# Masked keys by GpSimd instead of DMA, five normalisations moved to GpSimd, and values formed by head parity, in a four-block transformer kernel

## The reference

```python
x = _L0_xcond_ref(x, cond, ctx, ...)    # norm, attention over ctx (1 head), router of 3 experts, gate
x = _L1_xcond_ref(x, cond, ctx, mask, ...)  # norm, self attention, norm, cross attention, norm, MLP
x = _L2_xcond_ref(x, cond, ctx, ...)    # the same with other details; ctx is normalised too
x = _L3_xcond_ref(x, cond, ctx, ...)    # the same with rotary queries and keys

# inside blocks 1 to 3, self attention (cross attention takes keys and values from ctx):
q, k, v = split(xn @ qkv_w + qkv_b)               # 16 heads of 8 features
w = softmax(einsum('bqhd,bkhd->bhqk', q, k) * scale)
out = einsum('bhqk,bkhd->bqhd', w, v) @ proj_w
x = x + gate * out
```

## Time and profile before

| | us |
|---|---|
| median of 3 runs | 2580.94 |
| lowest, highest | 2578.9, 2584.88 |
| the profiled execution | 2582.11 |
| its span, from first to last instruction | 2580.3 |

### The profile page before, as it was taken

The page is one execution under the profiler, slowest core; times in us unless marked ns, Lnnn a source line. Parts: engine busy times, 40 slices in busy tenths (PEclk is TensorE's granted clock), DMA queues, the critical chain, the costliest instruction groups (busy, mean ns, idle before and its releaser), DMA issues.

```text
span 2580.3 us, 79116 instructions
## 1 busy us (share of the span) xinstructions
PE 2315.9 (90%) x32156; PEld 1821.8 (71%) x32156; DVE 2078.1 (81%) x4845; ACT 1904.0 (74%) x4567; POOL 70.0 (3%) x100
## 2 busy tenths in 40 slices
PE   3989899999989999899999889998899999998897
PEld 3767677767776777767777667776677777776675
DVE  4697878878788887788877988878887888787885
ACT  2678767777777877678777777777786887776875
POOL 0000000000000000000000000000000000000000
PEclk9999999999999999999999999999999999999998
DMA  6100000000100000000000000010001000000000
GB/s 135 39 14 21 14 22 26 31 16 13 30 21 30 15 17 27 27 23 15 18 30 30 13 20 20 27 30 13 20 20 31 30 15 15 26 18 22 12 12 16
DMA packets 99458, 62.90 MB, mean 24 GB/s; under 512 B 32992, under 2 KB 94368, under 8 KB 99104
## 3 DMA queue, kind: packets, MB, share of 16 engines
q1 hardware_dynamic: 90592, 57.80, 7.6%
q10 hardware_dynamic: 8512, 0.03, 0.2%
HBM read 28.31 MB, written 4.29 MB: 13 GB/s over the span
## 4 chain that ended last, share of the span: by engine, by line
PE 45%; DVE 31%; ACT 11%; DMA 5%; issue 4%; SPq 2%; DVEq 0%; ACTq 0%
PE pair L806 9%; DVE mx L1020 8%; DVE wide L1022 7%; PE pair L843 7%; PE pair L783 6%; PE pair L828 5%; PE pair L859 4%; PE pair L864 4%; DVE wide L1016 3%; DVE stats L900 2%; DMA wide<-probs_by_expert 2%; ACT xn L936 2%; PE pair L878 2%; DVE wide L918 2%; DVE x L1050 2%
## 5 line engine op out<-in xcount | busy, mean ns | idle before, releaser
L966 ACT ACTIVATE wide<-pair 128x1024 f32<-128x1024 f32 x384 | 390.3, 1022 | 122.6 <-PE pair L843 119.5
L1020 DVE TENSOR_REDUCE mx<-pair 128x16 f32<-128x1024 f32 x320 | 389.5, 1217 | 82.2 <-PE pair L828 81.5
L843 PE MATMUL pair<-konst,wide 128*128 128x128 f32 x3072 | 405.7, 276 | 54.8 <-DVE wide L1022 42.0
L843 PEld LDWEIGHTS pair<-konst,wide 128*128 128x128 f32 x3072 | 342.5, 142 | 120.5 <-DVE wide L1022 78.4
L1022 DVE TENSOR_TENSOR wide<-pair,mx 128x1024 f32<-128x1024 f32 x320 | 391.9, 1225 | 10.9
L936 ACT ACTIVATE xn<-pair,table 128x64 f32<-128x64 f32 x896 | 287.7, 406 | 46.3 <-PE pair L927 44.9
L828 PE MATMUL pair<-km,qT 32*64 32x256 f32 x6144 | 221.5, 394 | 94.5 <-DMA km<-kT 24.8
L959 ACT ACTIVATE vb<-pair 64x128 f32<-64x128 f32 x768 | 207.2, 270 | 38.1 <-PE pair L813 23.2
L918 DVE TENSOR_SCALAR wide<-x,mv,rstd 128x128 f32<-128x128 f32 x640 | 191.3, 343 | 50.9 <-ACT rstd L911 47.3
L828 PEld LDWEIGHTS pair<-km,qT 32*64 32x64 f32 x6144 | 125.8, 133 | 149.6 <-issue 20.6
L859 PEld LDWEIGHTS pair<-wide,vb 128*32 128x32 f32 x12288 | 184.0, 110 | 53.9 <-issue 17.6
(11 more groups left out here) (219 smaller groups left out, 4315.0 us busy)
## 6 DMA issues: line engine op xcount, KB each, us to landing
km<-kT SPq DMA_DIRECT2D x768, 32.0 KB, 1.8
wide<-probs_by_expert SPq DMA_DIRECT2D x32, 256.0 KB, 2.9
x<-in_x_dram SPq DMA_DIRECT2D x32, 128.0 KB, 2.4
ctx<-in_ctx_dram SPq DMA_DIRECT2D x32, 128.0 KB, 2.3
wide<-probs_by_expert SPq DMA_DIRECT2D x32, 128.0 KB, 3.2
out_dram<-x SPq DMA_DIRECT2D x32, 128.0 KB, 1.9
w0e<-in_L_xcond_e_w_dram SPq DMA_DIRECT2D x4, 384.0 KB, 5.8
w1fc<-in_L_xcond_fc_w_dram SPq DMA_DIRECT2D x2, 256.0 KB, 4.9
```

What stands on the lines that cost most here:

```text
L843: ins = pe.transpose(b[:, t:t + 128], G.ss[:, 2 * c + rr, a:a + 128], ident)
L966: act.activation(G.pT[:, :, 4 * c:4 * c + 4, :].rearrange("k p h q -> k p (h q)"), two_banks(name)[:].rearrange("k (p n) -> k p n", p=2), ...
L1020: dve.tensor_reduce(top, heads(s), AX_X, ALU.max).then_inc(*tick("dve", ("max", G.n, tag, c)))
```

## The change

1. The masked keys are made by GpSimd: `pool_keys` (step `kp`) multiplies `kT` by a column of 0s and 1s (`K_OWN + j` in `konst`) into each of the four copies, in place of the four DMAs. `keys_in` is gone; `pe_scores` and `copied_before` wait for GpSimd's tick ("keys").
2. `pool_apply` does the two `tensor_scalar` of the normalisations 1b, 2b, 3b, 2c and 0 on GpSimd. The other six stay on VectorE.
3. `pe_values` forms values per sequence and head parity: eight products of 128 x 64 with 64 columns (a strided view of the weights), odd heads into partitions 64 to 127. `act_values` then needs two ScalarE instructions of 64 x 256.
4. The costs given to the steps, and `hop`, are other numbers, and all of `PLACES` is another order. Of its lines, those of the steps `km` or `kp` and `s` of tag 1s stand for the rest (one number a visit).

```diff
-PE_MM, PE_TURN, PE_SCORES, PE_MIX = 0.44, 0.12, 1.05, 1.95
+PE_MM, PE_TURN, PE_SCORES, PE_MIX = 0.45, 0.12, 1.07, 1.915
...
-    "km1s": "185 234 275 276 995 1105 1279 1395 1971 2089 2255 2369 2947 3067 3241 3353 3932 4049 4217 4329 4911 5020 5197 5317 5891 6005 6174 6290 6870 6982 7153 7266",
-    "s1s": "188 251 279 306 1002 1112 1284 1399 1981 2093 2264 2378 2965 3073 3242 3361 3946 4051 4227 4341 4926 5031 5204 5321 5904 6015 6185 6302 6885 6992 7157 7277",
...
+    "s1s": "158 247 290 317 1002 1224 1272 1328 1979 2202 2253 2310 2959 3182 3231 3289 3939 4164 4214 4271 4919 5141 5195 5252 5901 6122 6173 6232 6880 7098 7150 7207",
+    "kp1s": "155 232 268 280 991 1210 1240 1318 1971 2199 2222 2299 2949 3174 3208 3278 3929 4152 4187 4261 4911 5139 5165 5241 5889 6112 6131 6220 6870 7092 7125 7194",
...
-NK = K_ONE + 3 * PV
+K_OWN = K_ONE + 3 * PV
+NK = K_OWN + 4
...
+    k[p, K_OWN + p % JH] = 1
...
         def pe_values(pe, G, tag, src, w):
 
             b = claim(pe, (G.n, tag, "v"))
-            for p in range(TT):
-                ins = pe.matmul(b[:, p * D:(p + 1) * D], src[:, p * 128:(p + 1) * 128], w, start=True, stop=True)
+            parity = w.rearrange("f (g e d) -> f g e d", e=2, d=HD)
+            for b2 in range(2):
+                for p in range(TT):
+                    tok, a = (2 * p + b2) * S, (b2 * TT + p) * S
+                    for e in range(2):
+                        ins = pe.matmul(b[S * e:S * e + S, a:a + S].rearrange("k (g d) -> k g d", d=HD), src[:, tok:tok + S],
+                                        parity[:, :, e, :], start=True, stop=True)
             ins.then_inc(*tick("pe", ("mm", (G.n, tag, "v"))))
 
         def pe_scores(pe, G, tag):
 
             pe.wait_ge(*done("qT", G.n, tag))
-            pe.wait_ge(keys_in[G.stream], 16 * JH * copies(G, tag))
+            pe.wait_ge(*done("keys", G.n, tag))
...
+        on_pool = ("1b", "2b", "3b", "2c", "0")
...
+        def pool_apply(pool, G, tag):
+
+            x, _, mv, rstd, out = norm_of(G, tag)
+            pool.wait_ge(*done("rstd", G.n, tag))
+            for t in range(TT):
+                pool.tensor_scalar(out[:, t, :], x[:, t, :], mv[:, t, 0:1], rstd[:, t:t + 1], ALU.subtract, ALU.mult)\
+                    .then_inc(*tick("pool", *([("normed", G.n, tag)] if t else [])))
...
-            src = tile(name)[:, 0:T].rearrange("k (h o e d) -> k h o e d", h=TT * HP // 2, o=2, e=2)
-            for b2 in range(2):
-                dst = G.vb[:, b2].rearrange("k p m (t w) -> k (p m) t w", t=3)
-                for e in range(2):
-                    end = [("free", name), ("vb", G.n, tag)] if (b2, e) == (1, 1) else []
-                    act.activation(dst[64 * e:64 * e + 64, :, 0:3:2, HD * e:HD * e + HD], src[64 * b2:64 * b2 + 64, :, :, e, :],
-                                   ACT.Copy).then_inc(*tick("act", *end))
+            src = tile(name)[:, 0:T].rearrange("k (h o d) -> k h o d", o=2, d=HD)
+            dst = G.vb[:].rearrange("k b p m (t w) -> k (b p m) t w", t=3)
+            for e in range(2):
+                end = [("free", name), ("vb", G.n, tag)] if e else []
+                act.activation(dst[S * e:S * e + S, :, 0:3:2, HD * e:HD * e + HD], src[S * e:S * e + S], ACT.Copy).then_inc(*tick("act", *end))
...
-        def sp_keys(sp, G, tag):
-
-            n = copies(G, tag)
-            if n > 1:
+        def pool_keys(pool, G, tag):
+
+            if copies(G, tag) > 1:
                 before, last = (G.n - NS, "3x") if tag == "1s" else (G.n, attentions[attentions.index(tag) - 1])
-                sp.wait_ge(*done("mm", (before, last, "s", 1)))
-            sp.wait_ge(*done("kT", G.n, tag))
+                pool.wait_ge(*done("mm", (before, last, "s", 1)))
+            pool.wait_ge(*done("kT", G.n, tag))
             for j in range(JH):
-                sp.dma_start(G.km[j:128:JH, j, :], G.kT[j:128:JH, :]).then_inc(keys_in[G.stream], 16)
+                pool.tensor_scalar(G.km[:, j, :], G.kT[:], konst[:, K_OWN + j:K_OWN + j + 1], None, ALU.mult)\
+                    .then_inc(*tick("pool", *([("keys", G.n, tag)] if j == JH - 1 else [])))
...
-            put(G, "ap" + tag, "dve", DVE_APPLY, lambda dve: dve_apply(dve, G, tag), "rstd" + tag)
+            if tag in on_pool:
+                put(G, "ap" + tag, "pool", 2 * 0.45, lambda pool: pool_apply(pool, G, tag), "rstd" + tag)
+            else:
+                put(G, "ap" + tag, "dve", DVE_APPLY, lambda dve: dve_apply(dve, G, tag), "rstd" + tag)
...
-            put(G, "km" + tag, "sp", 0.3, lambda sp: sp_keys(sp, G, tag), "kT" + tag, *last[-1:], lag=2.2)
+            put(G, "kp" + tag, "pool", 4 * 0.59, lambda pool: pool_keys(pool, G, tag), "kT" + tag, *last[-1:])
```

More of the change, by code:

```diff
@@ L543, in build @@
         probs_in = [sem(f"probs_spread_{n}") for n in range(NS)]
-        keys_in = [sem(f"masked_keys_copied_{n}") for n in range(NS)]
         pool_done = sem("pool_steps_done")
@@ L549, in build @@
         route_out, route_in = sem("route_table_written"), sem("route_table_spread")
-        nums = [s.num for s in (*sems.values(), *stored, *x_loaded, *ctx_loaded, *probs_out, *probs_in, *keys_in)]
+        nums = [s.num for s in (*sems.values(), *stored, *x_loaded, *ctx_loaded, *probs_out, *probs_in)]
         assert sorted(nums) == list(range(min(nums), max(nums) + 1))
@@ L989, in dve_rotary @@
             dve.wait_ge(*done(name, G.n, tag))
-        def sp_keys(sp, G, tag):
-            n = copies(G, tag)
-            if n > 1:
+        def pool_keys(pool, G, tag):
+            if copies(G, tag) > 1:
                 before, last = (G.n - NS, "3x") if tag == "1s" else (G.n, attentions[attentions.index(tag) - 1])
-                sp.wait_ge(*done("mm", (before, last, "s", 1)))
-            sp.wait_ge(*done("kT", G.n, tag))
+                pool.wait_ge(*done("mm", (before, last, "s", 1)))
+            pool.wait_ge(*done("kT", G.n, tag))
             for j in range(JH):
-                sp.dma_start(G.km[j:128:JH, j, :], G.kT[j:128:JH, :]).then_inc(keys_in[G.stream], 16)
+                pool.tensor_scalar(G.km[:, j, :], G.kT[:], konst[:, K_OWN + j:K_OWN + j + 1], None, ALU.mult)\
+                    .then_inc(*tick("pool", *([("keys", G.n, tag)] if j == JH - 1 else [])))
         def copied_before(engine, G, tag):
             if copies(G, tag) > 1:
-                engine.wait_ge(keys_in[G.stream], 16 * JH * (copies(G, tag) - 1))
+                before, last = (G.n - NS, "3x") if tag == "1s" else (G.n, attentions[attentions.index(tag) - 1])
+                engine.wait_ge(*done("keys", before, last))
         def dve_scores(dve, G, tag, c, masked):
@@ L1384, in put_block0 @@
             put(G, "kT0", "act", ACT_256, act_k0, "k0", gives=[("0", "k")])
-            put(G, "s0", "pe", 0.45, lambda pe: pe_scores0(pe, G), "xn0", "kT0", takes=[(("0", "s"), 1)])
+            put(G, "s0", "pe", 0.4, lambda pe: pe_scores0(pe, G), "xn0", "kT0", takes=[(("0", "s"), 1)])
             put(G, "sub0", "dve", 0.5, lambda dve: dve_sub0(dve, G), "s0", gives=[("0", "s")])
-            put(G, "exp0", "act", 0.3, lambda act: act_scores0(act, G), "sub0", table=EXP_TABLE)
-            put(G, "probs0", "dve", 0.65, lambda dve: dve_probs0(dve, G), "exp0")
+            put(G, "exp0", "act", 0.2, lambda act: act_scores0(act, G), "sub0", table=EXP_TABLE)
@@ L1392, in put_block0 @@
             put(G, "ev0", "act", ACT_256, lambda act: act_out(act, G, ("0", "ev"), G.rot[:], 0.0, ("ev", n)), "evid0", gives=[("0", "ev")])
-            put(G, "lg0", "pe", 0.8, lambda pe: pe_route(pe, G), "ev0", takes=[(("0", "lg"), 1)])
+            put(G, "lg0", "pe", 0.82, lambda pe: pe_route(pe, G), "ev0", takes=[(("0", "lg"), 1)])
             put(G, "rsub0", "dve", 3 * DVE_SMALL, lambda dve: dve_route_sub(dve, G), "lg0", gives=[("0", "lg")])
-            put(G, "rexp0", "act", 0.22, lambda act: act_route(act, G), "rsub0", table=EXP_TABLE)
+            put(G, "rexp0", "act", 0.12, lambda act: act_route(act, G), "rsub0", table=EXP_TABLE)
@@ L1396, in put_block0 @@
             put(G, "route0", "dve", 3 * DVE_SMALL, lambda dve: dve_route(dve, G), "rexp0")
-            put(G, "tr0", "pe", 0.1, lambda pe: pe_turn_route(pe, G), "route0", takes=[(("0", "pr"), 1)])
-            put(G, "pr0", "act", 0.25, lambda act: act_turn_route(act, G), "tr0", gives=[("0", "pr")])
-            put(G, "spread0", "sp", 2.5, lambda sp: sp_spread(sp, G), "pr0", lag=2.3)
+            put(G, "tr0", "pe", 0.12, lambda pe: pe_turn_route(pe, G), "route0", takes=[(("0", "pr"), 1)])
+            put(G, "pr0", "act", 0.16, lambda act: act_turn_route(act, G), "tr0", gives=[("0", "pr")])
@@ L1400, in put_block0 @@
+            put(G, "spread0", "sp", 3.6, lambda sp: sp_spread(sp, G), "pr0", lag=1.8)
             for k in range(NE + 1):
@@ L1483, in put_visit @@
                     norm(G, "2c", ["mix" + c], done("mm", (n, c, "o")), None, None, G.cn, 1)
-            put(G, "store", "sp", 0.1, sp_store, "x3", lag=2.0)
```

(1 more changed line is left out.)

47 lines of the change are left out of this document (24 added, 23 removed), and 486 rows, old and new, of the table PLACES.

## The result

The kernel after takes 2611.53 us (median of 3 runs, 2607.5 to 2616.54), 1.0124 times the kernel before [1.0096, 1.0152]: 30.6 us slower. The forecast was 2535, faster. The profiled execution took 2616.54 us, its span 2614.8.

A forecast was written before the change was run, and what follows sets the result against it. PE, 91% busy in the steady stretch, was taken as nearest to full. On 2582.1 us, -62 + 55 - 25 + 12 - 12 - 15 = -47 gave 2535 us, range 2450 to 2620.

The forecast's parts named there:

- Keys, -62: PE's idle time ahead of the score matmuls: GpSimd batches of 2.4 us instead of 4.2 by DMA give back 62 us.
- Normalisations, +12: Five normalisations per visit take longer on GpSimd and sometimes wait behind a key batch: 12 us lost (0 to 40).
- VectorE, -25: VectorE loses 109 us of normalisations; of PE's 67 us of waits ending at VectorE, 25 come back (0 to 45).
- Values, +55 and -12: Value products: PE's 16 narrower passes cost 55 us (bounds 38 to 94); ScalarE's two evictions instead of four gain 12.
- Rival (c): Keys leave the path, but PE's extra work for values is at its upper bound, +94: no net change, 2582; chance 0.14.
- Router and order, -15: VectorE's 32.5 us wait for router probabilities, with keys off SP and priced nearer their time: 15 us gained (0 to 30).
- Rival (b): GpSimd's list becomes what the scores wait for, key copies at 1.05 us or more: +50, 2632; chance 0.18.
- The sum: All terms added on the profiled execution of 2582.1 us: -47, giving 2535 us for the whole kernel.

The follow-up runs named there:

- e15: The kernel after with a key batch as four two-input GpSimd multiplications of 128 x 256 instead of the scalar form; 2554.94 us, 0.9914 times the kernel before.
- e16: As e15, with each GpSimd normalisation also as two two-input instructions of 128 x 256; 2535.50 us, 0.9838 times the kernel before.
- e3: The kernel after with the key copies made by DMA from SP again, in the new order; 2605.45 us, 1.0098 times the kernel before.
- e8: The kernel before, in its old order, with only the five normalisations moved to GpSimd; 2598.77 us, 1.0065 times the kernel before.
- e5: All three changes of operations (keys, normalisations, values) in the order and step costs of the kernel before; 2786.69 us, 1.0798 times the kernel before.
- e1: The kernel after with the five normalisations back on VectorE, in the new order; 2649.12 us, 1.0274 times the kernel before.
- e9: The kernel after with a key batch as one two-input GpSimd multiplication of 128 x 1024; 2596.38 us, 1.0071 times the kernel before.
- e6: The kernel before, in its old order, with only the values and their eviction changed; 2584.57 us, 1.0015 times the kernel before.
- e4: The kernel after with all operations of the kernel before, so only the new order stays; 2668.45 us, 1.0349 times the kernel before.

## Why the prediction went wrong, point by point

**Keys, -62: the price failed, the mechanism held.** The step that failed is the upper bound of one copy: "GpSimd's two-input add 0.728 from above". It supposed, without a row for it, that GpSimd does a one-input instruction no slower than a two-input one of the same shape, as VectorE does (0.293 against 0.424). On GpSimd it is the other way round: 0.922 with a column as scalar, 0.85 with a constant, 0.61 with two inputs (medians). So a batch took 3.62 us and not 2.4, outside the bounds of 1.2 to 2.9, and the gain at the scores was 24 us. With the price that the sum used (0.61, e15 and e16) the scores idle 28 us, where the prediction said "near 30", and e15, which differs from after in the form of these copies alone, is 57 us faster. The Trainium skill ("GPSIMD Engine Reference", Engine selection) has one-input elementwise work on GpSimd at roughly line rate; 0.922 against VectorE's 0.293 doesn't agree, and the measurement decides.

**Normalisations, +12: the size failed.** The bounds of half a normalisation, 0.342 to 0.728, missed 0.792. More than that, the wait behind a key batch was taken at 0.3 us of which 15% counts, some 7 us in all; measured, PE stood 45.5 us for GpSimd's normalisations. Some half of it goes with the key batches and the other half is the longer normalisation itself: without keys on the list it is 24.5 us in e3 and 20.4 in e8. The text named them as standing behind the keys on GpSimd's list, and then priced that with a share of busy time (26%). Such a share says nothing of bunching: in e5 three batches stood ahead of one normalisation, with GpSimd at rest before.

**VectorE, -25: not shown.** The four waits of the earlier trace rows that were added up to 67 us come to 10.8 + 1.8 + 7.9 + 3.6 = 24 in after, 43 less. But the order changed too, and e8, in which the normalisations alone leave VectorE, has 39.8 + 8.7 + 6.9 + 6.9 = 62 of the 67 left, the first of them here (PE's waits, e8):

```profile
PE pair L843 <- DVE wide L1032: 39.8, 62, 2.3
```

In the old order, then, freeing VectorE gave back 5 us of these waits. In the new one they are 78 us with the normalisations on VectorE (e1) and 24 without, so there it counts. That GpSimd holds VectorE up was right: line 926 takes 0.396 us in the mean, where line 918 took 0.343 before, and its longest is 0.87. The Trainium skill ("SBUF — State Buffer", Who interferes with whom) calls it an exclusive lock that makes the later one wait fully; the 2.1 us beside a 1.9-us instruction in e9 agree.

**Values, +55 and -12: too dear.** Together they were forecast at +43. Start to next start (timeline of PE, after):

```profile
135.81 0.69 PE L818 MATMUL pair<-w1qkv,xn 128*64 128x64 f32 x16
136.42 1.09 PE L849 MATMUL pair<-konst,wide 128*128 128x128 f32 x8
```

That is 0.61 us, against 0.44: 0.17 more and not 0.30, 33 us in all. The steady stretch of e6 has 24 us more PE busy than the earlier trace rows:

```profile
97.00:2540.00 2443.00, 2253.86 (x33696) 1755.21 (x33695) 2016.55 (x4629) 1786.61 (x4044) 67.43 (x93) 1.00 0.07 22
```

And "nearly all of it counts" was wrong: e6's total rose by 4 us, no more than can be told from none, as PE's idle time fell by 24 (table). ScalarE's part was right: two evictions of 0.374 us, 63.5 us less (143.7 against 207.2). Rival (c) is gone with this.

**Router and order, -15: not a term that can be added.** The old operations lose 88 us in the new order, the new ones 175 in the old one (e5 against after). The prediction counted what the new order leaves between key step and scores, in steps; for what else stands on GpSimd's list it made no such count. The router's wait itself fell from the 32.5 us of the earlier trace rows to 6.6 (VectorE's waits, after), but what PE had of that can't be told apart from the order:

```profile
DVE kT L1237 <- DMA wide<-probs_by_expert: 6.6, 10, 1.4
```

That the order of before was drawn up with 2.5 us for the key step, as the prediction has it, no run shows either.

**Rival (b)** had the right place, GpSimd's list, but the wrong threshold. It was to decide from 1.05 us a copy, where a batch is as long as the DMAs; at 0.92 it came out slower all the same. The comparison with 4.2 us looks only at the keys' own way, and not at what a batch costs those behind it, which was felt at 3.62 us already.

**The sum.** With the price that it had for a key copy, the kernel does come out where it said: e16 gives 2535.5 us. That the last digits agree is luck. A normalisation still takes 1.24 us there and not 0.90, the transposes idle 38.3 us, the values were cheaper than forecast (2250.0 us of PE busy in a steady stretch of 2393, where the prediction had 2285 of 2396), and the clock, which the sum left out, gave some back. These misses cancel.

**Open.** Why the scalar form is dearer on GpSimd than the two-input form isn't known: the column accounts for 0.08 of some 0.3 us. How much of the 88 us of e4 is the places of the steps and how much the PSUM banks that the new costs choose wasn't taken apart. Two key instructions of 128 x 512, and an order made for e16's prices, were not tried.

## What to carry to other kernels

Price work that moves to GpSimd from a row of the same form on GpSimd, and where there is none, measure that one instruction first: an upper bound taken from another form was what turned this forecast around. Once two kinds of steps share an in-order list, price what stands ahead of each in the list, and not the list's busy share; and don't read the worth of one operation from undoing it alone, since in an order that doesn't fit this measures the misfit too. Beside a busy VectorE, four short GpSimd instructions (e15) were better here than one long one (e9), though the long one is faster in itself.

## What the runs showed of the hardware that was not expected

- GpSimd's scalar form was slower than its two-input form: 128 x 256 in 0.92 us with a column, 0.85 with a constant, 0.61 with two inputs of which one is broadcast; half the size, 128 x 128 with two columns, in 0.79.
- A long two-input GpSimd instruction can hold VectorE for about its whole length (0.34 and 0.43 became 2.1 us at the longest, beside 1.9).
- TensorE's clock goes with the idle time that a change makes. PE does the same instructions in after and in e16; e16 has 59 us less idle time, and at a mean clock of 0.997 instead of 0.988 PE's busy time is 23 us shorter as well. An estimate from these means: with 1 as the upper and 0.5 as the lower level, 63 us of after and 15 of e16 lie at the lower one, and 48 us less of half speed are worth 24. So of the 82 us between their spans more than a quarter is clock.
